# Two selective scans on VectorE: states written to SBUF and multiplied in place, one more pair turned from ScalarE, and output stores awaited later

## The reference

```python
def step(state, xs):                      # state: batch x 1024 x 16
    d_t, B_t, C_t, u_t = xs
    dA = exp(d_t[..., None] * A)
    state = state * dA + (d_t * u_t)[..., None] * B_t[:, None, :]
    y_t = einsum('ben,bn->be', state, C_t)
y = (y + D * u) * silu(z);   x = x + tanh(g_xattn) * y
# then, on x: layernorm, choose 256 rows of each 2048 by a router's score,
# attention and a gated MLP on these rows, written back over x + tanh(g_ffn) * norm(x)
```

## Time and profile before

| | |
|---|---|
| median of 3 runs (lowest to highest) | 2764.08 us (2761.74 to 2764.15) |
| the profiled execution: its time, and the span from first to last instruction | 2760.83 us, 2759.1 us |
| first scan, first to last instruction of GpSimd's | 158.7 to 931.5 us |
| routing of sequences 0 and 1 | 936.9 to 1024.6 us, its last stores to about 1032 us |
| second scan | 1215.0 to 2061 us |
| busy over the span | PE 91%, DVE 72%, ACT 59%, POOL 57% |

### The profile page before, as it was taken

The page is one execution under the profiler, slowest core; times in us unless marked ns, Lnnn a source line. Parts: engine busy times, 40 slices in busy tenths (PEclk is TensorE's granted clock), DMA queues, the critical chain, the costliest instruction groups (busy, mean ns, idle before and its releaser), DMA issues. The chain is left out here.

```text
span 2759.1 us, 38288 instructions
## 1 busy us (share of the span) xinstructions
PE 2518.9 (91%) x13528; PEld 1845.1 (67%) x13528; DVE 1983.6 (72%) x2516; ACT 1617.6 (59%) x3482; POOL 1578.1 (57%) x882
## 2 busy tenths in 40 slices
PE   8969999999999549889899999999988799999998
PEld 3346666666666318556688888888754676488853
DVE  5779999999999766569999999999978535110000
ACT  4578888888888443377887788888752205100000
POOL 1269999999999510038898899889861000000000
PEclk9989999999999759999999999999998899999999
DMA  7732253432522497762352353353319740344442
GB/s 281 250 103 82 62 150 84 140 107 70 161 69 62 181 373 277 276 197 80 120 183 86 116 194 106 115 177 115 114 52 341 264 148 22 122 146 152 153 153 99
DMA packets 252624, 412.55 MB, mean 150 GB/s; under 512 B 50833, under 2 KB 134801, under 8 KB 249873
## 3 DMA queue, kind: packets, MB, share of 16 engines
q1 hardware_dynamic: 238928, 353.98, 39.9%
q10 hardware_dynamic: 12160, 51.39, 4.6%
q0 software_dynamic: 1344, 4.72, 0.5%
HBM read 325.09 MB, written 84.94 MB: 149 GB/s over the span
## 5 line engine op out<-in xcount | busy, mean ns | idle before, releaser
L763 POOL TENSOR_TENSOR s_x<-s_hp,k_bC 128x1024 f32<-128x1024 f32 x272 | 643.2, 2367 | 67.1 <-DVE s_hp L1297 66.5
L739 POOL TENSOR_TENSOR s_x<-s_du,k_bB 128x1024 f32<-128x1024 f32 x254 | 601.2, 2375 | 40.2 <-PE s_py L888 24.1
L888 PE MATMUL s_py<-k_ident,s_x 128*128 128x128 f32 x4096 | 519.0, 273 | 17.5 <-POOL s_x L763 16.9
L888 PEld LDWEIGHTS s_py<-k_ident,s_x 128*128 128x128 f32 x4096 | 462.5, 142 | 26.3 <-POOL s_x L763 21.2
L1222 ACT ACTIVATE s_pA<-s_delta,k_negA 128x512 f32<-128x512 f32 x512 | 333.9, 682 | 165.0 <-DVE s_x L1274 159.8
L1990 PE MATMUL l_p<-l_hT,l_ring 128*128 128x256 f32 x1792 | 390.3, 381 | 2.0 <-ACT l_hT L2095 1.4
L1990 PEld LDWEIGHTS l_p<-l_hT,l_ring 128*128 128x128 f32 x1792 | 342.3, 191 | 49.9 <-ACT l_hT L2095 1.6
L1222 ACT ACTIVATE s_x<-s_delta,k_negA 128x512 f32<-128x512 f32 x512 | 340.6, 710 | 0.0
L1100 ACT ACTIVATE s_xT<-s_duT,k_BT 128x128 f32<-128x128 f32 x1024 | 336.4, 389 | 0.1
L1297 DVE TENSOR_TENSOR_SCAN s_hp<-s_x,s_pA 128x512 f32<-128x512 f32 x256 | 309.7, 1212 | 32.0 <-ACT s_x L1222 18.0
L1297 DVE TENSOR_TENSOR_SCAN s_hp<-s_x,s_carry,s_pA 128x512 f32<-128x512 f32 x256 | 324.3, 1269 | 11.4 <-PE s_pA L870 4.4
(11 more groups left out here) (239 smaller groups left out, 3714.6 us busy)
## 6 DMA issues: line engine op xcount, KB each, us to landing
k_bC<-scratch_xd SPq DMA_DIRECT2D x32, 1024.0 KB, 11.7
scratch_ug<-p_ug ACTq DMA_DIRECT2D x16, 1024.0 KB, 4.3
k_u<-scratch_ug SPq DMA_DIRECT2D x64, 256.0 KB, 3.4
k_bB<-scratch_xd SPq DMA_DIRECT2D x32, 512.0 KB, 8.2
s_gy<-scratch_ug SPq DMA_DIRECT2D x64, 256.0 KB, 4.4
s_xt<-in_x SPq DMA_DIRECT2D x64, 256.0 KB, 4.7
scratch_x<-s_xt SPq DMA_DIRECT2D x64, 256.0 KB, 3.2
r_x<-scratch_x SPq DMA_DIRECT2D x32, 512.0 KB, 10.4
```

The source lines that it names most:

```text
L739: pool.tensor_tensor(out=x[:, 4 * g:4 * g + n], in0=du[:, s % 2:s % 2 + 1].broadcast_to([P, n, HALF]), in1=bB[:, into:into + n], op=ALU.mu ...
L763: pool.tensor_tensor(out=x[:, 2 * i:2 * i + 2], in0=hp_of(s, i), in1=bC[:, 2 * i:2 * i + 2], op=ALU.mult).then_inc(pool_hc, 1)
L888: last = nc.tensor.matmul(py[:, a], x[:, n, a * P:(a + 1) * P], ident[:], is_transpose=True, start=False, stop=n == NS - 1 and a == HALF / ...
```

## The change

- **States of VectorE's pairs in SBUF.** The scan of pairs 0, 2, 4 and 6 (where VectorE multiplies) writes to `x[:, n]`, over its own added term, and no longer to PSUM. `times_C` on VectorE then multiplies `x` by `bC` in place: both inputs and the output are in SBUF.
- **Waits that follow from it.** `release` waits for the scan alone for every pair. In units with `th == 0` VectorE's product waits until ScalarE has copied the carry (`carried`), and stands behind the second scan of the next pair and not between its two scans.
- **One more turned pair in the second scan.** `TURNED` becomes (1, 3, 7) and `SCALED` (5,) there: pair 1's `du * B` comes from eight more scalings of 128x128 on ScalarE and a transpose, and no longer from a matmul with diagonals. `PARTS_AT` and `PARTS_AHEAD` say in which slot of the unit the 24 scalings (16 before) are issued. GpSimd makes half as many diagonals there. The first scan keeps (3, 7) and (1, 5).
- **Output stores of the first routing awaited later.** 12 of the 16 buffers of `x2` now lie in `bC` and `bB`, which live on beyond the stage; SyncE waits for the stores from the other 4 buffers at the end of routing, and for the 12 in the attention layer, before it reloads `bC` and `bB` (`out_left`).

```diff
-TURNED, SCALED = (3, 7), {0: (1, 5), SPAN: (1, 5)}
+        self.out_left = nc.alloc_semaphore(f"c{first}_out_left")
+TURNED, SCALED = {0: (3, 7), SPAN: (1, 3, 7)}, {0: (1, 5), SPAN: (5,)}
...
-PARTS_AT = (8, 8, 10, 12, 14, 16, 16, 5)
+PARTS_AHEAD = {0: (0, 5), SPAN: (3, 8)}
+PARTS_AT = {0: (8, 8, 10, 12, 14, 16), SPAN: (11, 12, 16, 18, 20, 24)}
...
-        free = len(states_by_pool(first))
-        diagB = bB[:, free:free + ND_B].rearrange("p n (a q) -> p n a q", q=P)
+        diagB = sb("diagB", [P, ND_B, HALF // P, P])
...
             def make_b(s, i):
                 if s or i > 1:
-                    before, pair = (s, i - 2) if i > 1 else (s - 1, i - 2 + NPAIR)
-                    if pair in vec_pairs(first, before):
-                        pe.wait_ge(vec_hc, after_vec(before, pair))
-                        if parts(before)[1] == 0:
-                            pe.wait_ge(carried, after_carry(before, pair))
-                    else:
-                        pe.wait_ge(scanned, NS * before + 2 * pair + 2)
+                    pe.wait_ge(scanned, NS * s + 2 * i - 2)
...
             def release(s, i):
...
-                if i in vec_pairs(first, s):
-                    act.wait_ge(vec_hc, after_vec(s, i))
-                    if ends:
-                        j = 2 * (i % 2)
-                        nc.scalar.activation(kept, pA[:, j:j + 2, HALF - 1], ACT.Copy).then_inc(carried, 1)
-                        act.wait_ge(carried, after_carry(s, i))
-                else:
-                    act.wait_ge(scanned, NS * s + 2 * i + 2)
-                    if ends:
-                        nc.scalar.activation(kept, hp_of(s, i)[:, :, HALF - 1], ACT.Copy).then_inc(carried, 1)
+                act.wait_ge(scanned, NS * s + 2 * i + 2)
+                if ends:
+                    states = hp_of(s, i) if i in pool_pairs(first, s) else x[:, 2 * i:2 * i + 2]
+                    nc.scalar.activation(kept, states[:, :, HALF - 1], ACT.Copy).then_inc(carried, 1)
...
                 dve.wait_ge(scanned, NS * s + 2 * i + 2)
-                nc.vector.tensor_tensor(x[:, 2 * i:2 * i + 2], pA[:, j:j + 2], bC[:, 2 * i:2 * i + 2], ALU.mult).then_inc(vec_hc, 1)
+                if parts(s)[1] == 0:
+                    dve.wait_ge(carried, after_carry(s, i))
+                nc.vector.tensor_tensor(x[:, 2 * i:2 * i + 2], x[:, 2 * i:2 * i + 2], bC[:, 2 * i:2 * i + 2], ALU.mult).then_inc(vec_hc, 1)
...
-                out = pA[:, n % 4]
+                out = x[:, n]
                 if i in pool_pairs(first, s):
                     out = hp_of(s, i)[:, n % 2]
...
                     scan(s, 2 * i)
-                    times_C(s, i - 1)
+                    if parts(s)[1]:
+                        times_C(s, i - 1)
                     scan(s, 2 * i + 1)
+                    if not parts(s)[1]:
+                        times_C(s, i - 1)
...
+    if late:
+        for kept in (keep.bC, keep.bB):
+            flat = kept[:].rearrange("p n l -> p (n l)").rearrange("p (j d) -> p j d", d=DI)
+            beside += [flat[:, j] for j in range(kept.shape[1] * HALF // DI)]
+    OWN = BUFS - len(beside)
+    own = sb("x2", [P, OWN, DI])
+    x2 = [own[:, j] for j in range(OWN)] + beside
...
-            for j in range(BUFS):
-                sp.wait_ge(out_done[j], 16 * len(range(j, SPAN * TILES, BUFS)))
+            for j in range(OWN):
+                sp.wait_ge(out_done[j], 16)
...
+                sp.wait_ge(chosen_rows.out_left, 16 * ((keep.bC.shape[1] + keep.bB.shape[1]) * HALF // DI))
                 for g in range(NS // 4):
                     keep.load_states(sp, t, SPAN, g, kept)
```

More of the change, by code:

```diff
@@ L75, in __init__ @@
         self.ropes = ctx.enter_context(nc.sbuf_tensor(f"c{first}_ropes", [P, SPAN, 2 * DH], F32))
-TURNED, SCALED = (3, 7), {0: (1, 5), SPAN: (1, 5)}
+        self.out_left = nc.alloc_semaphore(f"c{first}_out_left")
+TURNED, SCALED = {0: (3, 7), SPAN: (1, 3, 7)}, {0: (1, 5), SPAN: (5,)}
 def states_by_pool(first):
-    return [n for n in range(NS) if n // 2 not in TURNED + SCALED[first]]
+    return [n for n in range(NS) if n // 2 not in TURNED[first] + SCALED[first]]
 def quad_place(first, g):
@@ L98, in sb @@
             return ctx.enter_context(nc.sbuf_tensor("k_" + name, shape, F32))
-        self.bB = sb("bB", [P, max(len(states_by_pool(first)) + 2 * len(SCALED[first]) for first in SCALED), HALF])
+        self.bB = sb("bB", [P, max(len(states_by_pool(first)) for first in SCALED), HALF])
         self.bC = sb("bC", [P, NS, HALF])
@@ L428, in scan_stage @@
     negA, ident, tg, BT = keep.negA, keep.ident, keep.tg, keep.BT
-    scaled = SCALED[first]
-    from_pe = tuple(sorted(TURNED + scaled))
+    turned, scaled = TURNED[first], SCALED[first]
+    from_pe = tuple(sorted(turned + scaled))
+    NT = 2 * len(turned)
     NF, ND_B = 2 * len(from_pe), 2 * len(scaled)
@@ L804, in _ @@
                     begin(s + 1)
-                if last_tile and scaled:
-                    make_diagonals(chunk(s) + 1, scaled[0])
+                if last_tile and 1 in scaled:
+                    make_diagonals(chunk(s) + 1, 1)
                 if fill:
@@ L813, in _ @@
                 times_C(s, 5)
-                if last_tile and scaled:
-                    make_diagonals(chunk(s) + 1, scaled[1])
+                if last_tile and 5 in scaled:
+                    make_diagonals(chunk(s) + 1, 5)
                 quad(s + 1, 1)
@@ L861, in make_b @@
                 for n in (2 * i, 2 * i + 1):
-                    if i in TURNED:
-                        k = 2 * TURNED.index(i) + n % 2
+                    if i in turned:
+                        k = 2 * turned.index(i) + n % 2
                         pe.wait_ge(xT_ready, NT * s + k + 1)
@@ L1226, in _ @@
                         copy_du(0)
-                        make_states(0, 0, PARTS_AT[-1])
+                        make_states(0, 0, PARTS_AHEAD[first][1])
                     if i == 0:
@@ L1382, in sem @@
         return nc.alloc_semaphore(f"r{first}_" + name)
-    x2 = sb("x2", [P, BUFS, DI])
+    late = first == 0
+    beside = []
+    if late:
[5 more added lines that the diff above has]
+    x2 = [own[:, j] for j in range(OWN)] + beside
     scrap = sb("scrap", [P, 4, DI])
@@ L1415, in route_stage @@
     p_pos = ctx.enter_context(nc.psum_tensor(f"r{first}_ppos", [P, 1], F32))
-    late = first == 0
     if not late:
@@ L1451, in load @@
             def load(k):
[L1452 to L1455, removed]
+                sp.dma_start(x2[k], t[f"x2_{first}"][k * P:(k + 1) * P, :]).then_inc(x_in[k], 16)
             def load_weights(j):
@@ L1539, in store @@
                 act.wait_ge(base_ready, k + 1)
-                act.dma_start(t["out"][row(k):row(k) + P, :], x2[:, buf(k)[0]]).then_inc(out_done[buf(k)[0]], 16)
+                act.dma_start(t["out"][row(k):row(k) + P, :], x2[k]).then_inc(out_done[k] if k < OWN else chosen_rows.out_left, 16)
             def finish_u(k):
```

21 lines of the change are left out of this document (10 added, 11 removed).

## The result

The changed kernel takes 2914.12 us, the median of four runs (2912.26 to 2918.7); the kernel before takes 2762.98 us, also the median of four, on the same chip. The ratio is 1.055, with a 95% interval from 1.0531 to 1.0568, so the change costs about 151 us. The prediction was 2967 us, with a range from 2890 to 3080. The profiled execution of the changed kernel took 2918.7 us.

The account below looks back on a forecast made before the run. The prediction took GpSimd to bound the first scan, VectorE close behind, and TensorE to lead the second. It summed 2760.8 + 114 + 94 - 5 = 2964 us, with 3.3 us for the runs' median 2967 us; range 2890 to 3080.

Parts of the forecast that it names:

- The block: In both scans, VectorE's product with two SBUF inputs and GpSimd's instructions delay each other: +114 and +94 us.
- GpSimd's term: GpSimd's instructions lengthen by 1.016 us per VectorE product: 114 us in the first scan, 130 in the second.
- VectorE's term: VectorE's product waits for GpSimd: 1.01 us each in the first scan, 0.93 in the second; 113 and 119 us.
- Second scan: VectorE takes the lead at 893.4 us of work, loses 24.8 us of waits for TensorE: stretch 916 us, +94.
- The turned pair: Second scan: TensorE's 29 us less and ScalarE's 80 us more both hidden: 0, upper bound +10 us.
- The carry: VectorE's product waiting for ScalarE's carry copy, in half of the units, costs 0; bound +10 us, shared with ScalarE's bursts.
- The stores: End of first routing: -5 us, bounds 2 and 6.6; attention layer's first DMA some 5 us after the last store.
- Price of the instructions in SBUF: VectorE in both scans: products +6 us, scans writing to SBUF -6.5 us, taken as 0.
- A: Both scans: GpSimd waits, VectorE doesn't; +114 and +44 us, 2917 us in all; chance 0.17.
- B: Both scans: the engines lock in step, VectorE waits 1.4 us per product: 3059 us; chance 0.20.
- C: Nothing blocks in the scans; TensorE's relief in the second saves VectorE 24.8 us of waits: 2734 us; chance 0.06.
- D: Neither block nor relief: ScalarE's 80 us delay exponentials by TensorE's gain; within 5 us of 2764; chance 0.02.

Follow-up runs that it names:

- experiment 5: Kernel before with VectorE's states in SBUF and product in place, but its second input read from PSUM, C left out; 2806.17 us, ratio 1.0162.
- experiment 2: Kernel before with only VectorE's states in SBUF and the in-place product; pair 1 by diagonals and stores as before; 2917.59 us, ratio 1.0565.
- experiment 7: Changed kernel with VectorE's product between the two scans of the next pair in all units, still waiting for the carry; 2942.77 us, ratio 1.0655.
- experiment 3: Kernel before with only pair 1 additionally turned in the second scan; 2801.83 us, ratio 1.0144.
- experiment 4: Kernel before with only the output stores of the first routing awaited later; 2759.11 us, ratio 0.9991.
- experiment 6: Kernel before with pair 1 turned in the second scan from pair 3's scaled tiles, without its own eight scalings; 2749.68 us, ratio 0.9953.

## Why the prediction was right, and where its sizes were off

**The block.** The term that decided was the right one, in both directions. Experiment 5 removes it with one operand and experiment 2 has it alone. The Trainium skill's rule (SBUF — State Buffer, Who interferes with whom) is borne out for both sides, by 1.24/2.26 us and 2.21 us in the timeline above; the 8.00 us record goes beyond it.

*GpSimd's term* was 1.016 us for each product. In the first scan it is (851.69 - 748.83)/112 = 0.92, where 748.83 us is what the kernel before has over its scan from 165 to 931 us. In the second it is (838.46 - 734.90 + 5)/128 = 0.85 (before from 1223 to 2061 us). The row that I took is a meeting in which VectorE had only just begun; on average, I take it, less of its instruction is left.

*VectorE's term* was 1.01 and 0.93 us. It is (819.89 - 739.18)/112 = 0.72 in the first scan and (877.87 - 785.28)/128 = 0.72 in the second. (By the records of the products alone it is 0.79: 1984 - 1199 ns. The busy time of the engine has the slightly shorter scans in it too, and counts overlaps once.) This is the step that was most mis-sized: I took arrivals spread evenly over GpSimd's instruction, half of it times its busy share. Experiment 7 shows that the mean moves by 0.18 us with the product's place alone, so the arrivals are not spread evenly. Which arrangement gives 0.72 was not settled.

**First scan:** +114 predicted, +104.3 measured, GpSimd the bound, as said. Nearly the whole difference is the 0.92 in place of 1.016 (103 against 114).

**Second scan:** +94 predicted, +53.1 measured. VectorE is the bound, as said. Its term is 119 - 92.6 = 26 us too large. The other 14 us are idle time: I let it give up the 24.8 us of waits for TensorE, and it gave up 38.6, from 52.7 to 14.1 us over the scan. The reason was off too. I put these 24.8 us down to TensorE's relief by the turned pair, and experiment 2, which has no relief, has only 18.3 us of idle time in its second scan (1325.4 to 2217 us). So the idle time goes mostly because VectorE's own work has become longer, and of the relief no more than the 4 us between 18.3 and 14.1 are left. That is the second step that was off.

**The turned pair** was taken at 0, and in the changed kernel it is 0 (experiment 2 against the changed kernel, 896.1 and 896.3 us). The reason that carried the term, that VectorE covers it, fits. I also wrote that ScalarE's 80 us would fit if the stretch stayed at 822 us, since `release` no longer waits for the products. That was not tested: in experiment 3 they cost 40 us, but there `release` still waits for the products, and no run has the turned pair, `release` waiting for the scan only, and no block. So which of the two hides the scalings in the changed kernel, VectorE as the bound or the earlier `release`, stays open, and the 0 may owe something to luck. ScalarE's waits there are these:

```profile
ACT s_x L1210 <- DVE s_hp L1288: 64.5, 46, 2.5
ACT s_carry L1110 <- DVE s_x L1288: 36.4, 28, 3.2
```

They are the two longest of the changed kernel's second scan and both end with a scan; those for line 1274 in the earlier trace rows are gone, as predicted.

**The carry:** taken at 0, and 0.2 us in the changed kernel. With the product between the two scans in all units it is 9.1 us (experiment 7), and 52.4 where ScalarE must wait for the product as well (experiment 5).

**The stores:** -5 predicted. The first routing is 6.8 us shorter and the layer 7.8 us longer, with its first loads later. From the start of the first scan to that of the second the changed kernel takes 1163.2 us and experiment 2, with the stores as before, 1160.5, so what the stage gained was given back in the next. I let the layer's first loads give back 1.6 us; in experiment 4 the layer gives back 3.3 of 7.0 us, and alone the step is 2.7 us. Why the layer is 7.8 us longer in the changed kernel and 1.4 in experiment 2, which has the stores as before, is not settled. The sign that I gave for it was also wrong: the layer's first DMA goes out 1.4 us after the last store is issued, where it was 7.6 before, and not some 5; taking 5 us off 7.6 would have left 2.6.

**Price of the instructions in SBUF:** taken at 0. The shortest product is 1189 ns and experiment 5's 1206, against 1199 from PSUM. The scans are 15 to 17 ns shorter, but this isn't shown to be the price of writing to SBUF, as the scans with unchanged operands lost 7 and 18 ns too. The 0 stands. The Trainium skill's shorter fixed cost from SBUF (VectorE: DVE Perf Modes, The TRN2 errata) doesn't show in the product; the same section says that its SBUF figure for VectorE is too low for a single operation.

**The rivals.** A, 2917 us, is nearest in time to the 2914 that came, and for the wrong reason: it has VectorE wait for nothing, and VectorE waits 0.72 us. B's lock above 1.11 us didn't come. C and D are excluded by experiment 2, where the block alone costs the whole loss. C's relief of 25 us was also too large: with nothing to pay for it, it is 11 us in experiment 6.

**The signs.** VectorE's product at 1.98 us on average was said to be near 2.2, GpSimd's two at 2.76 and 2.50 near 2.7 each. Lines 868 and 870 (862 and 864 in the changed kernel) have the 1280 and 1536 matmuls foretold. GpSimd is full in the first scan, and at 94% in the second (838.46 of 892 us).

## What to carry to other kernels

Before moving an operand from PSUM to SBUF on VectorE, count how often it would then read two SBUF inputs while GpSimd is busy. Price each meeting on both engines, at up to the rest of the other's instruction, and take the engine that bounds the stage. Don't count all of the time that an engine spends in waits as room for more work: of some 80 us added to ScalarE beside 166.5 us of such waits, the waits gave up only 37 (experiment 3). Ask first whether the wait itself goes.

## What was not expected of the hardware

The engine that loses can lose more than once: a VectorE product of 1.2 us took 8.00 us while GpSimd began five instructions of 1.24 us one after the other, once in 240. While a VectorE product is held, its record runs on as busy time and not as idle: VectorE's busy time rose by 172.7 us with the same instructions, so the busy share alone would have shown an engine with more work. GpSimd's instructions were stretched by at most about 1.0 us each, whatever their own length: 128x1024 products from 2.37 to at most 3.41 us, 128x512 ones (lines 723, 727 and 771) from 1.28 to at most 2.29, and the diagonals (line 753) from 0.63 to at most 1.64.
